# Two pre-activation conv layers, 8 x 32 x 512 x 512: x1 kept in the output tensor and accumulated onto by the stores

## The reference, cut to what is computed

```python
x = x + L0(gn(x), w0, b0)      # 3x3 conv, inputs, weights and output quantised
x = x + L1(gn(x), w1, b1)
# gn: group normalisation, 16 groups of 2 channels, over the whole image
# L1:
feat = einsum('bihw,oi->bohw', x, conv_w) + conv_b        # 1x1 conv, 32 -> 32
filt = einsum('kh,bchw,lw->bckl', Ph, feat, Pw)           # 5x5 averages of feat
out  = depthwise_conv(feat, filt)                         # each plane by its own 5x5 filter
```

## Time and profile before

| | us |
|---|---|
| median of 3 runs (6186.45 to 6190.99) | 6187.13 |
| the profiled execution | 6187.55 |
| its span, first to last instruction | 6185.9 |

### The profile page before, as it was taken

How to read it: one execution, slowest core, us unless ns; L and a number is a source line. 1 busy time by engine, 2 the same in 40 slices (tenths; PEclk the granted TensorE clock), 3 DMA queues, 4 the chain that set the end, 5 groups by cost and what they waited for, 6 DMA issues and landing times.

```text
span 6185.9 us, 112158 instructions
## 1 busy us (share of the span) xinstructions
PE 4916.9 (79%) x43630; PEld 3222.5 (52%) x43798; DVE 5284.7 (85%) x5934; ACT 3360.9 (54%) x2005; POOL 889.3 (14%) x1444
## 2 busy tenths in 40 slices
PE   1767676767676779349989989989899899899899
PEld 0111111111111112138878878878788788788787
DVE  6787878787878787659989989989899899899898
ACT  1656565646564649235545545545455455455454
POOL 0000000000000001102212212112112121122122
PEclk9888788878888889679999999999999999999999
DMA  8999999999999999389999999999999999999998
GB/s 259 301 280 307 287 300 287 303 286 294 299 301 298 297 286 299 100 182 257 244 251 251 250 252 252 251 249 257 246 260 243 256 255 250 256 249 251 252 255 195
DMA packets 617611, 1615.46 MB, mean 261 GB/s; under 512 B 81338, under 2 KB 82618, under 8 KB 580282
## 3 DMA queue, kind: packets, MB, share of 16 engines
q1 hardware_dynamic: 239298, 640.73, 41.7%
q0 software_dynamic: 162240, 537.03, 27.1%
q10 hardware_dynamic: 215488, 429.94, 25.8%
HBM read 1068.55 MB, written 538.84 MB: 260 GB/s over the span
## 4 chain that ended last, share of the span: by engine, by line
DVE 43%; issue 7%; DMA 3%; PE 2%; ACTq 1%; POOL 0%; SPq 0%; ACT 0%; DVEq 0%; another core or an unknown queue 0%; POOLq 0%
DVE c_z L1003 16%; DVE c_xr L1039 16%; DVE c_feat L1029 12%; DMA c_xr<-x_scratch 3%; PE c_tps L1083 1%; ACTq L859 1%; PE c_cps L1063 0%; POOL c_feat L922 0%; SPq L887 0%; PE c_cps L1065 0%; PE c_cps L1064 0%; ACT c_z L969 0%; DVEq L1002 0%; SPq L872 0%
## 5 line engine op out<-in xcount | busy, mean ns | idle before, releaser
L1083 PE MATMUL c_tps<-c_feat,c_tt 123*128 123x256 f16 (+1 forms) x20736 | 2377.0, 273 | 13.8 <-DVE c_xr L1039 10.7
L1083 PEld LDWEIGHTS c_tps<-c_feat,c_tt 123*128 123x128 f16 (+1 forms) x20736 | 1992.1, 97 | 275.0 <-issue 15.6
L987 ACT ACTIVATE c_feat<-c_cps 122x1024 f16<-122x1024 f32 x576 | 822.5, 1428 | 1352.1 <-PE c_cps L1065 1352.1
L1039 DVE SCALAR_TENSOR_TENSOR c_xr<-c_tps,c_xr 57x1024 f32<-57x1024 f32 (+1 forms) x1152 | 1403.2, 1218 | 158.6 <-DMA c_xr<-x_scratch 125.7
L443 PE MATMUL b_ps<-b_xq,w0main 128*128 128x512 bf16 x2904 | 918.4, 419 | 656.9 <-ACT b_q L401 484.5
L969 ACT ACTIVATE c_z<-c_x,c_rs 128x976 f16<-128x976 f32 x576 | 1156.6, 2008 | 275.5 <-PE c_tps L1083 169.1
L1003 DVE SCALAR_TENSOR_TENSOR c_z<-c_x,c_rs,c_z 128x976 f16<-128x976 f32 x576 | 1087.1, 1887 | 105.3 <-ACT c_z L969 92.9
L1063 PE MATMUL c_cps<-w_high,c_z 128*128 128x128 f16 x4608 | 822.1, 222 | 421.5 <-DVE c_z L1003 385.6
L936 POOL DMA_DIRECT2D out_dram<-c_xr x1152 | 667.4, 580 | 2892.5 <-DVE c_xr L1039 2827.9
L401 ACT ACTIVATE b_q<-b_ps,q_bias 128x1024 int8<-128x1024 f32 x512 | 549.2, 1115 | 813.8 <-DVE b_x L521 745.5
L456 PE MATMUL b_ps<-b_xq,w0edge 64*32 64x512 bf16 x3048 | 931.3, 416 | 0.0
(11 more groups left out here) (129 smaller groups left out, 2267.0 us busy)
## 6 DMA issues: line engine op xcount, KB each, us to landing
x_scratch<-b_x POOLq DMA_DIRECT2D x256, 1024.0 KB, 12.3
c_xr<-x_scratch SPq DMA_DIRECT2D x576, 384.0 KB
out_dram<-c_xr POOLq DMA_DIRECT2D x576, 384.0 KB, 7.9
b_stream<-in_x_dram SPq DMA_DIRECT2D x672, 256.0 KB, 12.4
b_x<-in_x_dram ACTq DMA_DIRECT2D x276, 512.0 KB, 13.6
b_x<-in_x_dram SPq DMA_DIRECT2D x276, 512.0 KB, 11.7
c_tt<-table_scratch SPq DMA_DIRECT2D x64, 576.0 KB
c_xr<-x_scratch SPq DMA_DIRECT2D x512, 72.0 KB
```

The costliest lines, as they stand in the source:

```text
L987: act.activation(dst, cps[0:MAIN, s % 2, :, :].rearrange("p j (q o) -> p o q j", q=Q), ACT.Identity).then_inc(fh_done, 1)
L1039: last = dve.scalar_tensor_tensor(res, tps[PR * h:PR * h + n, s % 2, :, :], 1.0 / FS, res, ALU.mult, ALU.add)
L1083: last = pe.matmul(tps[:, s % 2, o % 4, :], tt[0:rows, o, tp, 2 * d:2 * d + 2, :].rearrange("k w m -> k (w m)"), feat[0:rows, (e * N + i) ...
```

## The change

1. `quantised_conv` stores x1 into the output tensor, laid out [b, c, h, w], not into a scratch tensor. A chunk now takes four DMAs of 32 partitions each.
2. `depthwise` loads its x1 tiles from the output tensor, in four DMAs of 32 partitions (partition order is now (q, c)), from SP's queue, at step 6 of a group. POOL waits for the load of tile j before the first store of group j, since the stores overwrite rows that the load reads.
3. There is no `load_xr`. DVE writes `tps` / 64 of one parity and ACT that of the other into `c_xr`, and the store adds to what lies in the output (`accum_op`). `c_xr` has four slots, each free again when its store has landed.
4. `z` has four slots; ACT's `high` runs two steps ahead and stands behind the high part of `feat`.
5. Small: the pointwise weights are laid out by DVE copies, and `rstd` is used as it is, without a copy by DMA.

```diff
-XR_SLOTS = 6
+XR_SLOTS = 4
+Z_SLOTS = 4
...
-        x1v = x1.rearrange("b (n j r) c w -> b n (r c) j w", j=JB, r=4)
-        STORE = 2 * 16
+        x1v = x1.rearrange("b c (n j r) w -> b n r c j w", j=JB, r=4)
...
-                    for h in range(2):
-                        rows = slice(JB // 2 * h, JB // 2 * (h + 1))
-                        pool.dma_start(x1v[b, n, :, rows, :], xt[:, s, rows, :]).then_inc(x1_stored[s], 16)
+                    for r in range(Q):
+                        pool.dma_start(x1v[b, n, r, :, :, :], xt[C * r:C * r + C, s, :, :]).then_inc(x1_stored[s], 16)
...
-        x1v = x1.rearrange("b h c (q w) -> b (c q) h w", q=Q)
+        x1v = out.rearrange("b c h (q w) -> b q c h w", q=Q)
...
-            eng.dma_start(xt[:, x_slot(e, j), lo:hi, :],
-                          x1v[2 * p + e + de, :, r0 + lo:r0 + hi, :]).then_inc(x1_loaded[x_slot(e, j)], 16)
+            for q in range(Q):
+                eng.dma_start(xt[C * q:C * q + C, x_slot(e, j), lo:hi, :],
+                              x1v[e + de::2][p, q, :, r0 + lo:r0 + hi, :]).then_inc(x1_loaded[x_slot(e, j)], 16)
...
             def group(p, e, j, pointwise, banded):
                 if not banded:
+                    load_x1(sp, p, e, 0)
+                    load_x1(sp, p, e, 1)
                     for g in range(4):
                         load_table(p, e, g)
                 for s in range(STEPS):
-                    if banded:
-                        load_xr(p, e, j - 1, s)
...
+                    if s == 6 and pointwise and (j + 2 < N or another(p, e)):
+                        load_x1(sp, p, e, j + 2)
...
+                if pointwise:
+                    pool.wait_ge(x1_loaded[x_slot(e, j)], loads_of(p, e, j) + START)
...
-                    pool.wait_ge(summed, count(p, e, TILES, m + 1) + START)
+                    pool.wait_ge(odd_out, count(p, e, TILES, m + 1) + START)
+                    pool.wait_ge(even_out, count(p, e, TILES, m + 1) + START)
                     for lo, hi in ((0, SPLIT), (SPLIT, n)):
                         pool.dma_start(out[e::2][p, 4 * s:4 * s + 4, r0 + lo:r0 + hi, :].rearrange("c h w -> h c w"),
-                                       xr_rows(m, lo, hi)).then_inc(stored[m % XR_SLOTS], 16)
+                                       xr_rows(m, lo, hi), accum_op=ALU.add).then_inc(stored[m % XR_SLOTS], 16)
...
+        def half_out(m, n, h):
+            return (xr_rows(m, 0, n).rearrange("h c (j p) -> h p c j", p=2)[:, 1 - h, :, :],
+                    tps[PR * h:PR * h + n, m % 2, :, :])
+
+        def wait_slot(eng, p, e, m):
+            eng.wait_ge(stored[m % XR_SLOTS], count(p, e, TILES // XR_SLOTS * 32, m // XR_SLOTS * 32) + 16)
...
                 for s in range(STEPS):
-                    nxt = convert_next(p, e, j, s)
-                    if nxt is not None:
-                        high(p, e, *nxt)
-                    act.wait_ge(conv_done, count(p, e, TILES, STEPS * j + s + 1) + START)
-                    dst = feat[0:MAIN, (e * N + j) % 2, 0, :, 1:FP - 1].rearrange("p o (q j) -> p o q j", q=Q)[:, :, :, 8 * s:8 * s + 8]
-                    act.activation(dst, cps[0:MAIN, s % 2, :, :].rearrange("p j (q o) -> p o q j", q=Q), ACT.Identity).then_inc(fh_done, 1)
-                if j + 2 < N or another(p, e):
-                    load_x1(act, p, e, j + 2)
+                    if pointwise:
+                        act.wait_ge(conv_done, count(p, e, TILES, STEPS * j + s + 1) + START)
+                        dst = feat[0:MAIN, (e * N + j) % 2, 0, :, 1:FP - 1].rearrange("p o (q j) -> p o q j", q=Q)[:, :, :, 8 * s:8 * s + 8]
+                        act.activation(dst, cps[0:MAIN, s % 2, :, :].rearrange("p j (q o) -> p o q j", q=Q), ACT.Identity).then_inc(fh_done, 1)
+                        nxt = ahead(p, e, j, s + 2)
+                        if nxt is not None:
+                            high(p, e, *nxt)
+                    if banded:
+                        m = STEPS * (j - 1) + s
+                        wait_slot(act, p, e, m)
+                        act.wait_ge(band_done, count(p, e, TILES, m + 1) + START)
+                        res, conv = half_out(m, rows_out(j - 1), 1)
+                        act.activation(res, conv, ACT.Identity, scale=1.0 / FS).then_inc(odd_out, 1)
...
+                        wait_slot(dve, p, e, m)
                         dve.wait_ge(band_done, count(p, e, TILES, m + 1) + START)
-                        dve.wait_ge(xr_loaded[m % XR_SLOTS], count(p, e, TILES // XR_SLOTS * 32, (m // XR_SLOTS + 1) * 32) + START)
-                        for h in range(2):
-                            res = xr_rows(m, 0, n).rearrange("h c (j p) -> h p c j", p=2)[:, 1 - h, :, :]
-                            last = dve.scalar_tensor_tensor(res, tps[PR * h:PR * h + n, s % 2, :, :], 1.0 / FS,
-                                                            res, ALU.mult, ALU.add)
-                        last.then_inc(summed, 1)
+                        res, conv = half_out(m, rows_out(j - 1), 0)
+                        dve.tensor_scalar(res, conv, 1.0 / FS, None, ALU.mult).then_inc(even_out, 1)
...
-                pe.wait_ge(summed, count(p, e, TILES, max(0, STEPS * i + s - 1)) + START)
+                pe.wait_ge(even_out, count(p, e, TILES, max(0, STEPS * i + s - 1)) + START)
+                pe.wait_ge(odd_out, count(p, e, TILES, max(0, STEPS * i + s - 1)) + START)
```

More of the change, by code:

```diff
@@ L114, in _ @@
                 sp.dma_start(k.b1col[rows, :], b1.rearrange("(o a) -> o a", a=1)).then_inc(loaded, 16)
-            sp.wait_ge(zeroed, 1)
-            for q in range(Q):
-                sp.dma_start(k.wf[q::Q, q, :], w1.rearrange("o c -> c o"), allow_slow_non_contiguous=True).then_inc(spread, 16)
         @block.gpsimd
@@ L616, in _, with filters @@
             dve.wait_ge(kept, 1 + START)
-def filters(nc, nb, k, sums, mean, rstd, rstd_cq, table_d, bias_d):
+def filters(nc, nb, k, sums, mean, rstd, table_d, bias_d):
     lots = -(-nb // 4)
@@ L747, in _ @@
         def _(sp):
-            for q in range(Q):
-                sp.dma_start(rstd_cq[q::Q, :], rstd[0:C, :]).then_inc(stored, 16)
             sp.wait_ge(tables_ready, 1)
@@ L759, in _, with depthwise @@
             sp.dma_start(table_d[nb, 0:1, 0:PR], blank[:, :]).then_inc(stored, 16)
-            sp.wait_ge(stored, 16 * (5 * lots + 1 + Q))
-def depthwise(nc, nb, k, x1, rstd, table_d, bias_d, out):
+            sp.wait_ge(stored, 16 * (5 * lots + 1))
+def depthwise(nc, nb, k, rstd, table_d, bias_d, out):
     with ExitStack() as ctx:
@@ L865, in _ @@
         def _(sp):
-            def load_xr(p, e, i, s):
-                m = STEPS * i + s
-                sp.wait_ge(stored[m % XR_SLOTS], count(p, e, TILES // XR_SLOTS * 32, m // XR_SLOTS * 32) + 16)
-                n, r0 = rows_out(i), ROWS_OUT * i
-                for lo, hi in ((0, SPLIT), (SPLIT, n)):
-                    sp.dma_start(xr_rows(m, lo, hi).rearrange("h c w -> h (c w)"),
-                                 x1[e::2][p, r0 + lo:r0 + hi, 4 * s:4 * s + 4, :].rearrange("h c w -> h (c w)")).then_inc(xr_loaded[m % XR_SLOTS], 16)
             def load_last_edge(p, e):
@@ L952, in scale_of, with ahead @@
             return rs[:, col:col + 1]
-        def convert_next(p, e, j, s):
-            if s < STEPS - 1:
-                return j, s + 1
-            return (j + 1, 0) if j + 1 < N or another(p, e) else None
+        def ahead(p, e, j, part):
+            if part < STEPS:
+                return j, part
+            return (j + 1, part - STEPS) if j + 1 < N or another(p, e) else None
+        def half_out(m, n, h):
[3 more added lines that the diff above has]
+            eng.wait_ge(stored[m % XR_SLOTS], count(p, e, TILES // XR_SLOTS * 32, m // XR_SLOTS * 32) + 16)
         @block.scalar
@@ L971, in group @@
             def group(p, e, j, pointwise, banded):
-                if not pointwise:
-                    return
                 if not banded:
-                    load_x1(act, p, e, 0)
-                    load_x1(act, p, e, 1)
                     high(p, e, 0, 0)
-                else:
+                    high(p, e, 0, 1)
+                elif pointwise:
                     act.wait_ge(band_done, count(p, e, TILES, STEPS * (j - 1)) + START)
                 for s in range(STEPS):
-                    nxt = convert_next(p, e, j, s)
-                    if nxt is not None:
-                        high(p, e, *nxt)
-                    act.wait_ge(conv_done, count(p, e, TILES, STEPS * j + s + 1) + START)
-                    dst = feat[0:MAIN, (e * N + j) % 2, 0, :, 1:FP - 1].rearrange("p o (q j) -> p o q j", q=Q)[:, :, :, 8 * s:8 * s + 8]
-                    act.activation(dst, cps[0:MAIN, s % 2, :, :].rearrange("p j (q o) -> p o q j", q=Q), ACT.Identity).then_inc(fh_done, 1)
@@ L988, in group @@
-                if j + 2 < N or another(p, e):
-                    load_x1(act, p, e, j + 2)
-            act.wait_ge(cleared, 1 + START)
```

(23 more changed lines are left out.)

37 lines of the change are left out of this document (16 added, 21 removed).

## The result

| | us |
|---|---|
| kernel after, median of 4 runs (5992.25 to 6001.27) | 5995.08 |
| kernel before, beside it | 6186.79 |
| ratio, 95% interval | 0.9694 (0.9678 to 0.9711) |
| span of the profiled execution | 5990.5 |

The account below looks back on a forecast made before the run. DVE was taken to bound the kernel within an image, passing to PE. From 6187.55 us: steps -182, changes of image -21, start -46, x1 store +64, together -185, so 6002 us; range 5920 to 6900.

Parts of the forecast that it names:

- The bound passes to PE: In depthwise, within an image, the bound moves from DVE (5.72 us a step) to PE (5.40): 182 us gained.
- The accumulating store: In depthwise, the store with the add costs twice the plain store, 2.5 to 3.5 us a step, still hidden.
- Rival 2: In depthwise, the accumulating store is dear and engines wait for it: about 7270 us at three times today's price; chance 0.31.
- The DMA engines: All DMA work in a depthwise step is 4.9 or 5.9 us; the lower side, below 5.40, was taken.
- rival 1: The DMA engines bound depthwise at 5.9 us a step, with ACT waiting for `c_x`: 6145 us; chance 0.18.
- Between images: At 7 changes of image in depthwise, a 23 us wait goes and a table wait of 20 comes: 21 us gained.
- The start: At the start of depthwise, the first x1 tile goes ahead of all other loads: 46 us gained.
- The store in the first part: In quantised_conv, the x1 store in DMAs of 32 partitions costs 0.5 us a chunk, 64 us in all.
- The sum: Over the whole kernel, the terms come to -185 us from 6187.55, so 6002 us.

Follow-up runs that it names:

- run 1: Kernel after with plain stores in place of the accumulating ones, so x1 is not added: 5955.96 us, ratio 0.9621.
- run 8: Kernel after with the tables loaded once only, images 1 to 7 using the filters of image 0: 5823.19 us, ratio 0.9414.
- run 2: Kernel after with SP's order at a change of image turned to table groups 0, 1, 2, then the x1 load, then group 3: 5986.91 us, ratio 0.9672.
- run 6: Kernel before, with SP waiting for the first x1 tile before it loads the tables at the start of depthwise: 6161.93 us, ratio 0.9948.
- run 5: Kernel before with only the x1 store of a chunk split into four DMAs of 32 partitions, same layout: 6185.07 us, ratio 0.9985.
- run 10: Kernel before with x1_scratch laid out [b, c, h, w], and the quarter stores, four x1 loads from ACT and residual loads that follow: 7336.12 us, ratio 1.1868.

## Why the prediction was right, point by point

**The bound passes to PE: right, and the step was better than I had it.** I read 5.29 from PE's own rows and then added a tenth, because banded starts beside DVE work stood 5.42 apart. That tenth was DVE's, not PE's. With DVE out of the way PE waits for nothing, and the step is 5.29. The term was -182 and measured -244. ACT's copy, taken at 1.43 from L987, costs 1.11.

**The accumulating store: right.** Forecast twice the plain store by its work, 2.5 to 3.5 us a step. Measured 2.8, 1.62 times plain (run 1). The time to land hardly grew (8.5 against 8.3 at the median), where I had allowed 16.6. The rule of the Trainium skill (Collectives: The Full Stack, The bandwidth ceiling) that an add costs its two reads would give about 2: this case, at 1.62, is below it. Rival 2, which carried 0.31, needed 1.9 times by the shares and failed there.

**The DMA engines: right within an image, in part open between images.** Within an image rival 1 was wrong. The shares add up to 1.01 and PE doesn't wait, and it doesn't run any faster at 0.85 (run 1), so the share is no measure of what is left. At the changes of image the bytes on SP's queue decide (run 8), and the work of the stores has a part in it (run 1). Rival 1's own sign, ACT waiting for `c_x` within the images, is not there: after the start there is one such wait, of 19.3 us.

**Between images: the term that was mis-sized.** I forecast that group 1 of the tables would be late, for its place behind the x1 tile, and the place and the waiting instruction were as forecast. At the first change PE wanted it 19.4 us after the tile was issued (I had 18), and had it after 47 (I had 34), so a tile and a group beside the stores were priced too low. Over the seven changes the wait is 167.5 us, 24 a change where I took 20. The larger miss is that I took away all 23 us that a change cost before, while the earlier trace rows puts only 125.7 / 7 = 18 of them down to the residual loads. Some 6 us a change stood beside that wait in the old kernel, and some 6 (41 / 7) stand in run 8, where no table is loaded. What they are is open, but for the two waits in run 8. And I had forgotten the clock, 1.6 us at the change read in run 2. By estimate 24 + 6 + 1.6 is the 31 us of a change. The term was -21 and measured +54. The remedy that follows from my account, the table ahead of the tile, was worth 2 us a change, since the wait moves on to the next thing behind the tile (run 2).

**The start: right in mechanism and size** (-46, measured -45), and run 6 shows in the old kernel that the first tile waited for the tables. The first tile took 26 us, not 21.

**The store in the first part: right in size by chance.** I priced the 32 partitions a DMA (+64) and didn't price the layout at all. Quarters alone ended the part 15 us earlier (run 5), quarters and layout 56 us later (run 10), and in the kernel after the two happened to come to +38 in place of +64. What is shown is that the layout does it, with a size that scatters between executions; that it is the distance of 1 MB between neighbouring channels' rows is the nearest reading, not tested apart from the shape.

**The sum** was right to 0.1% (6002 against 5995) because two misses of 62 and 75 us had opposite signs: the steps gained 62 us more than forecast and the changes of image lost 75 more. The first part, 26 us shorter than forecast, turned what was left, 13 us too long, into 13 too short. That is luck in the size of the terms. The prediction should be trusted for its bound and its rivals, not for the last 10 us.

## What to carry to other kernels

When a busy engine is relieved, read the next bound from the stretches where that next engine works alone; an interval measured beside the old bound still has the old bound in it. An accumulating store is a fair way to take an add off the compute engines: its worth here is that a plain copy can be given to ACT, and not the loads that it saves. A burst of loads that only comes now and then (tables at a change of image) is where a DMA queue shows its limit first, and an order that puts one load ahead only hands the wait to the load behind. And a gap that is taken away whole in a forecast should first be split into the waits that the trace names and the rest, which may well stay.

## What the runs showed of the hardware that I had not expected

- An accumulating store from POOL costs 1.62 times the DMA engine time of the same store without the add, in 16463 packets against 9117, and its landing is 1.3 us longer (8.5 against 7.2). POOL's own instruction goes from 0.58 us to 0.95 at the median:

```profile
L925 POOL DMA_DIRECT2D out_dram<-c_xr x114: 870/946/1192, 3201.4 to 3498.3; - x114
```

- A compute engine can stand still while it issues DMAs: some 21 us for four loads of 1 MB from ACT, 1665 us in all (run 10), where one load of 4 MB took 0.7, but 65.64 when it was issued right behind another one in the kernel before. That the queue was full is the nearest reading, not shown.
- The x1 loads of 512-byte runs went in packets of 2 KB from the old layout (26.40 MB in 12989) and of 509 bytes from the new one (28.02 MB in 55077), at 82 us of engine time a MB against 62. Which of the changed strides does it wasn't tried.
- The DMA share reads 1.01 with PE never waiting, and 0.85 with the same steps (run 1). It reads 1.06 with a single queue at work at 209 GB/s, so a full share doesn't say that a second queue would find no room.
